# A graph attention layer: one of eight groups of x comes in turned and is normalised along the partitions

## The chip, the cores and the metric

The kernel runs on 1 core of one Trainium2 chip. The metric is the time of one execution on the device in microseconds (us); less is better.

## The reference

```python
def _layernorm(x, axis=-1, eps=1e-05):
    m = jnp.mean(x, axis=axis, keepdims=True)
    v = jnp.var(x, axis=axis, keepdims=True)
    return (x - m) / jnp.sqrt(v + eps)

h = jnp.maximum(_layernorm(x, axis=-1), 0.0)      # x: (4096, 256) f32
q = h @ Wq.T + bq
k = h @ Wk.T + bk
v = h @ Wv.T + bv
a = q @ k.T * scale + adj + adj                   # adj: (4096, 4096) f32, scale = 1/16
out = x + softmax(a, axis=-1) @ v
```

## The kernel before, in words

x has 4096 rows of 256, in 8 groups (0 to 7) of 4 tiles of 128 rows. Wq and Wk are multiplied into one matrix G, so h itself, transposed (hT, features on the partitions), takes the place of the keys. Every product is made of three f32r products of an upper and a lower part (`split_product`, 12 matmuls for 2 tiles), so h, v and q exist as "hi" and "lo".

There are 16 blocks of 256 queries and, in each, 16 units of 256 keys: 256 steps. A step makes the scores of one unit (`scores`, 12 matmuls into PSUM bank s % 2), VectorE adds adj from a ring of 23 slots (`add_adj`), and keeps a running maximum (`running_max`). Behind it come the subtraction of the maximum on GpSimd, exp and p_hi on ScalarE, p_lo on VectorE, and the product with v (`weigh_values`), 22 steps later.

The first block is woven into a prelude in which the groups of x come in, one in each turn of a loop over g. The order on each engine is written by hand. For group g it does:
- SyncE's queue (SP): `load_x(g)` into one of three buffers, and two units of adj.
- VectorE: `tile_stats` (4 bn_stats) and `part_stats` (4 bn_aggr, var + eps), three turns ahead of use; GpSimd (`make_rstd`): the power -0.5, the negated mean, their product.
- ScalarE: `normalize`, 4 activations that scale and shift the rows.
- TensorE: `transpose_h`, 8 transposes into PSUM; ScalarE `h_hi` (Relu and rounding) and VectorE `h_lo` (the rest) write hT. The part number is the group's plus 1.
- TensorE: `project_v(g, pair)`; ScalarE `v_hi` (3 instructions), GpSimd `v_lo`.
- TensorE: `scores(2g)` and `scores(2g + 1)`; before scores(s) it waits for add_adj(s - 2), whose bank it writes.

`v_hi(g, pair)` waits for `v_lo(g - 1, pair)`, since both share the buffer v_full. `project_v(g, pair)` waits for `v_hi(g - 1, pair)`. The second block's queries are projected in the turn of group 7 (`project_q(1)`, `q_hi`, `q_lo`). How many maxima each turn makes stands in a table, half of them before and half after `add_adj(2g)`:

```python
MAXES = (1, 1, 2, 4, 6, 9, 12, 2 * GROUPS - 1)
...
first, behind = MAXES[g - 1], MAXES[g]
for s in range(first, (first + behind) // 2):
    running_max(s)
...
add_adj(2 * g)
for s in range((first + behind) // 2, behind):
    running_max(s)
```

Of the kernel before, what the change touches and what calls it, by code (L numbers as in the profile page):

```python
# [5 lines left out]
def graph_attention_kernel(nc, x_groups, adj_units, w_pack, b_pack, bv, out):  # L6
# [36 lines left out]
    MAXES = (1, 1, 2, 4, 6, 9, 12, 2 * GROUPS - 1)  # L43

    term_spill = [nc.dram_tensor(f"term_spill{n}", [TILES, P], f32, kind="Internal").ap() for n in range(2)]

    ctx = ExitStack()
    with ctx:
# [5 lines left out]

        hT = sb("hT", [P, 2, DB, TILES * P], f32r)
# [22 lines left out]
        with ExitStack() as later:  # L78
            x_third = sb("x_third", [P, GT, D], f32, later)
            sb("between", [P, 3, BANK], f32, later)  # L80
            v_full = sb("v_full", [P, 2, 2, D], f32, later)
# [73 lines left out]
        s_x = [sem(f"x_rows_loaded{b}") for b in range(XB)]  # L155
        s_adj = [sem(f"adj_loaded{n}") for n in range(RING)]
# [74 lines left out]
        def _(sp):  # L231
# [53 lines left out]
            sp.wait_ge(s_ht, DB * (GROUPS - 1))  # L285
# [26 lines left out]
        def _(pool):  # L312
# [5 lines left out]
            nc.gpsimd.memset(minus_half[:, :], -0.5)  # L318
            nc.gpsimd.memset(row_terms[:, :, :], 0.0).then_inc(s_tz, 1)
# [3 lines left out]
            def make_rstd(p):  # L323
# [7 lines left out]
                if p > 1:  # L331
                    pool.wait_ge(s_off, p - 1)
                nc.gpsimd.tensor_scalar(minus_mean[:, at], mean_var[:, g % XB, at, 0], -1.0, 0.0, ALU.mult, ALU.add)\
# [4 lines left out]
                    .then_inc(s_off, 1)  # L338

# [59 lines left out]
        def _(pe):  # L399
# [190 lines left out]
        def _(act):  # L590
# [69 lines left out]
            for g in range(1, GROUPS):  # L660
                v_hi(g, 0)
                if g + 1 < GROUPS:
# [3 lines left out]
                if g + 2 < GROUPS:  # L666
                    normalize(g + 3)
                v_hi(g, 1)

# [30 lines left out]
        def _(dve):  # L700
            def tile_stats(g, j):
                if g == 0:
                    dve.wait_ge(s_x0[j], 16)
                elif j == 0:
                    dve.wait_ge(s_mv, g + 1)
                    dve.wait_ge(s_x[g % XB], 16 * (g // XB + (1 if g % XB else 0)))
                nc.vector.bn_stats(stats[:, j], rows(g)[:, j]).then_inc(s_stat, 1)

            def part_stats(p):
                g, tiles = part_of(p)  # L710
                dve.wait_ge(s_stat, GT * g + tiles[-1] + 1)
                for j in tiles:
                    last = nc.vector.bn_aggr(mean_var[:, g % XB, j], stats[:, j])
# [5 lines left out]
                nc.vector.tensor_scalar(var_eps[:, at], mean_var[:, g % XB, at, 1], EPS, 1.0, ALU.add, ALU.mult)\  # L719
                    .then_inc(s_ve, 1)  # L720

            def normalize(p):
                g, tiles = part_of(p)
                dve.wait_ge(s_rstd, p + 1)
                for j in tiles[:by_vector(p)]:
                    last = nc.vector.tensor_scalar(rows(g)[:, j], rows(g)[:, j], mean_var[:, g % XB, j, 0:1],
                                                   rstd[:, g % XB, j:j + 1], ALU.subtract, ALU.mult)
                last.then_inc(s_norm2, 1)

# [119 lines left out]
            for g in range(1, GROUPS):  # L849
# [3 lines left out]
                if g + XB < GROUPS:  # L853
# [10 lines left out]
                add_adj(2 * g)  # L864
                for s in range((first + behind) // 2, behind):
# [61 lines left out]
```

## Time and profile before

| | us |
|---|---|
| median of 3 runs | 805.5 (805.5 to 805.56) |
| profiled execution, its time | 805.57 |
| its span, first to last instruction | 803.7 |
| PE (TensorE) busy | 798.9 (99%) |
| DVE (VectorE) busy | 560.1 (70%) |
| POOL (GpSimd) busy | 412.4 (51%) |
| ACT (ScalarE) busy | 355.9 (44%) |
| granted TensorE clock | 1.00 of full speed |

The profile is one execution recorded by the hardware profiler. The span leaves out what lies ahead of the first and behind the last instruction, 1.87 us here. PEld is the load of a matmul's stationary tile, which overlaps with the matmul ahead of it. Matmuls are pipelined: an instruction starts before the shown end of the one ahead, so for a row of matmuls the distance of the starts counts. An idle time stands in brackets at the instruction that follows it, with what it waited for.

### The profile page before, as it was taken

The page shows a single profiled execution, that of the slowest core. Times are in us where ns is not written, and L with a number is a line of the kernel's source. Part 1 is how long each engine was busy: PE and PEld are TensorE (multiplying, and loading weights), DVE is VectorE, ACT ScalarE, POOL GpSimd, SP SyncE. Part 2 cuts the span into 40 slices and gives each one's busy share as a digit, 9 for nine tenths or more (in the row PEclk, how much of TensorE's full clock was granted, in tenths as well). Part 3 has the DMA queues.
Part 4 walks back from the last instruction along what each step waited for, and adds up shares of the span by engine and source line. Part 5 has one row for each costly group of instructions (what it writes and reads, how often), then busy time and mean ns, then how long its engine had stood idle before and what let it go on. Part 6 is the DMA issues. An engine that isn't in the chain of part 4 may idle for free.

```text
span 803.7 us, 16607 instructions
## 1 busy us (share of the span) xinstructions
PE 798.9 (99%) x6642; PEld 797.1 (99%) x6642; DVE 560.1 (70%) x950; ACT 355.9 (44%) x636; POOL 412.4 (51%) x369
## 2 busy tenths in 40 slices
PE   9999999999999999999999999999999999999998
PEld 8999999999999999999999999999999999999998
DVE  7869666667666766767666766767676676676664
ACT  5764444434443443434344344434444434443375
POOL 4556638091652908256190734719174380926573
PEclk9999999999999999999999999999999999999999
DMA  8522433333332434334243433323333342333300
GB/s 264 193 77 73 118 81 125 93 112 105 100 106 80 135 94 113 93 99 114 85 125 93 121 93 99 110 92 112 97 109 105 88 128 86 110 104 97 90 27 14
DMA packets 46399, 83.57 MB, mean 104 GB/s; under 512 B 5617, under 2 KB 8305, under 8 KB 46321
## 3 DMA queue, kind: packets, MB, share of 16 engines
q1 hardware_dynamic: 45744, 81.71, 34.1%
q8 instruction: 52, 0.85, 0.4%
q10 hardware_dynamic: 576, 0.79, 0.3%
q14 instruction: 27, 0.21, 0.1%
HBM read 78.25 MB, written 4.23 MB: 103 GB/s over the span
## 4 chain that ended last, share of the span: by engine, by line
PE 98%; DVE 1%; ACT 0%; issue 0%; POOL 0%; DVEq 0%; ACTq 0%; POOLq 0%
PE ps L424 51%; PE ps L535 15%; PE ps L536 15%; PE ps L537 15%; PE ps L416 1%; PE ps L402 1%; PE ps L431 0%; ACT x_pair L613 0%; DVE x_res L813 0%; DVE qhl L740 0%; DVE x_res L802 0%; ACT qhl L622 0%; POOL rstd L327 0%; DVE p_lo L793 0%; ACT G L641 0%
## 5 line engine op out<-in xcount | busy, mean ns | idle before, releaser
L424 PE MATMUL ps<-qhl,hT 128*128 128x256 f32 x3072 | 407.8, 283 | 0.6 <-DVE qhl L740 0.6
L424 PEld LDWEIGHTS ps<-qhl,hT 128*128 128x128 f32 x3072 | 383.7, 190 | 0.8 <-DVE qhl L740 0.8
L535 PE MATMUL ps<-v,p_hi 128*128 128x258 f32 x1024 | 290.6, 284 | 0.3 <-DVE p_lo L793 0.3
L536 PE MATMUL ps<-v,p_lo 128*128 128x258 f32 x1024 | 288.9, 282 | 0.0
L537 PE MATMUL ps<-v,p_hi 128*128 128x256 f32 x1024 | 288.2, 281 | 0.0
L680 ACT CAST p_hi<-ps 128x512 fp32r<-128x512 f32 x256 | 150.5, 588 | 261.5 <-PE ps L537 259.8
L392 POOL TENSOR_TENSOR ring_a<-ring_a,m_row 128x512 f32<-128x512 f32 x179 | 226.7, 1310 | 16.1 <-ACT m_row L686 15.4
L748 DVE TENSOR_TENSOR ring_a<-ps,ring_a 128x512 f32<-128x512 f32 x179 | 123.5, 691 | 117.5 <-PE ps L424 116.4
L535 PEld LDWEIGHTS ps<-v,p_hi 128*128 128x128 f32 x1024 | 194.5, 190 | 0.9 <-DVE p_lo L793 0.7
L536 PEld LDWEIGHTS ps<-v,p_lo 128*128 128x128 f32 x1024 | 194.7, 190 | 0.0
L537 PEld LDWEIGHTS ps<-v,p_hi 128*128 128x128 f32 x1024 | 193.4, 189 | 0.0
L793 DVE TENSOR_TENSOR p_lo<-ps,p_hi 128x512 fp32r<-128x512 f32 x256 | 174.4, 682 | 12.8 <-ACT p_hi L680 12.8
L674 ACT ACTIVATE ps<-ring_a 128x512 f32<-128x512 f32 x179 | 108.2, 604 | 71.3 <-DVE p_lo L793 40.8
L375 POOL PARTITION_ALL_REDUCE m_row<-max_rows x14 | 15.2, 1088 | 215.4 <-DVE max_rows L771 215.4
L392 POOL TENSOR_TENSOR ring_b<-ring_b,m_row 128x512 f32<-128x512 f32 x77 | 97.5, 1310 | 0.4
L760 DVE TENSOR_TENSOR ps<-ps,ring_a 128x512 f32<-128x512 f32 x132 | 92.2, 698 | 3.8
L748 DVE TENSOR_TENSOR ring_b<-ps,ring_b 128x512 f32<-128x512 f32 x77 | 53.2, 691 | 50.8 <-PE ps L424 50.2
L379 POOL TENSOR_TENSOR m_row<-m_row,term_row 128x256 f32<-128x256 f32 x14 | 10.2, 729 | 101.7 <-issue 101.7
L674 ACT ACTIVATE ps<-ring_b 128x512 f32<-128x512 f32 x77 | 46.5, 604 | 31.1 <-DVE p_lo L793 16.3
L760 DVE TENSOR_TENSOR ps<-ps,ring_b 128x512 f32<-128x512 f32 x63 | 44.0, 698 | 1.9
L622 ACT ACTIVATE qhl<-ps,query_bias 128x256 fp32r<-128x256 f32 x32 | 13.4, 471 | 52.3 <-PE ps L424 52.3
L343 POOL TENSOR_TENSOR v<-v_full,v 128x512 fp32r<-128x512 f32 x16 | 19.7, 1234 | 26.1 <-ACT row_terms L635 26.1
(83 smaller groups left out, 334.3 us busy)
## 6 DMA issues: line engine op xcount, KB each, us to landing
ring_a<-in_adj SPq DMA_DIRECT2D x179, 256.0 KB, 2.7
ring_b<-in_adj SPq DMA_DIRECT2D x77, 256.0 KB, 2.7
x_res<-in_x SPq DMA_DIRECT2D x16, 256.0 KB, 3.0
out<-x_res SPq DMA_DIRECT2D x15, 256.0 KB, 2.0
x_pair<-in_x SPq DMA_DIRECT2D x5, 512.0 KB, 4.2
term_row<-term_spill SPq DMA_DIRECT2D x14, 128.0 KB, 3.2
x_third<-in_x SPq DMA_DIRECT2D x2, 512.0 KB, 5.0
w_all<-in_w ACTq DMA_DIRECT2D x2, 257.0 KB, 4.0
```

Source lines behind the costliest of these rows:

```text
L343: nc.gpsimd.tensor_tensor(v[:, t:t + 2, VW:VW + D], v_full[:, pair], v[:, t:t + 2, 0:D].bitcast(f32), ALU.subtract).then_inc(s_vlo, 1)
L375: nc.gpsimd.partition_all_reduce(m_row[:, :], max_rows.ap().rearrange("p i n -> p (i n)"), P, bass.bass_isa.ReduceOp.max).then_inc(s_max, 1)
L392: nc.gpsimd.tensor_tensor(slot_tiles(w), slot_tiles(w), m, ALU.subtract).then_inc(s_sub, 1)
L424: last = nc.tensor.matmul(dst, lhs(a, ib), rhs(c, ib), start=(n == 0), stop=(n == 3 * DB - 1))
L535: nc.tensor.matmul(ps[:, at, 0:VW], hi, v[:, n, 0:VW], start=(n == 0), stop=False)
L536: nc.tensor.matmul(ps[:, at, 0:VW], lo, v[:, n, 0:VW], start=False, stop=False)
L537: last = nc.tensor.matmul(ps[:, at, 0:D], hi, v[:, n, VW:VW + D], start=False, stop=(n == TILES - 1))
L674: nc.scalar.activation(ps[:, E_BANK + w % 2, :], slot(w), ACT.Exp, scale=2.0).then_inc(s_exp, 1)
L680: nc.scalar.copy(p_hi[:, w % PB], bank_tiles(E_BANK + w % 2)).then_inc(s_phi, 1)
L748: nc.vector.tensor_tensor(slot(s), ps[:, S_BANK + s % 2, :], slot(s), ALU.add).then_inc(s_add, 1)
L760: last = nc.vector.tensor_tensor(to, first, slot(s), ALU.max)
L793: nc.vector.tensor_tensor(p_lo[:, w % PB], bank_tiles(E_BANK + w % 2), p_hi[:, w % PB].bitcast(f32), ALU.subtract).then_inc(s_plo, 1)
```

## The change

Group 7 alone (LATE = 7) is no longer transposed on TensorE. The host hands over a second, transposed copy of its x (`in_xt`). Its plain rows are loaded into the place of hT's upper part for that group, and serve for the statistics; the turned rows are loaded into the place of the lower part. GpSimd puts 1/sqrt(var + eps) and the mean of the 512 rows side by side (`gather_moments`), VectorE turns them in blocks of 32x32, SP writes them to DRAM in four pieces (`spill_moments`) and reads each of the two rows of 512 values back to all 128 partitions (`load_key_row`, 256 KB each). GpSimd subtracts the means (`centre`), VectorE takes the maximum with 0 and multiplies (`scale_late`), ScalarE rounds to hi, VectorE writes lo (`late_lo`). In MAXES one maximum of the turn g = 3 moves to g = 4. In the code `make_rstd`, `normalize`, `transpose_h` and the PSUM forms of `h_hi` and `h_lo` are no longer called for group 7.

```diff
-def graph_attention_kernel(nc, x_groups, adj_units, w_pack, b_pack, bv, out):
+def graph_attention_kernel(nc, x_groups, x_turned, adj_units, w_pack, b_pack, bv, out):
...
-    MAXES = (1, 1, 2, 4, 6, 9, 12, 2 * GROUPS - 1)
-
+    LATE = GROUPS - x_turned.shape[0]
+    ROWS = 3
+    MAXES = (1, 1, 2, 3, 6, 9, 12, 2 * GROUPS - 1)
+
+    row_spill = [nc.dram_tensor(f"row_spill{n}", [2 * GT, P], f32, kind="Internal").ap() for n in range(GROUPS - LATE)]
...
+            h_plain = sb("h_plain", [P, 2, DB, TILES * P], f32, unsplit)
...
-            sb("between", [P, 3, BANK], f32, later)
+            key_rows = sb("key_rows", [P, ROWS, GT * P], f32, later)
...
+        def key_row(g, a):
+            n = 2 * (g - LATE) + a
+            return key_rows[:, n % ROWS, :].rearrange("p (one n) -> p one n", one=1).broadcast_to([P, DB, GT * P])
+
+        def rows_loaded(g, a):
+            n = 2 * (g - LATE) + a
+            return s_row[n % ROWS], 16 * (n // ROWS + 1)
+
+        def x_tile(g, j):
+            if g < LATE:
+                return rows(g)[:, j]
+            return h_plain[:, 0, j // 2, (g * GT + j % 2 * 2) * P:(g * GT + j % 2 * 2 + 2) * P]
...
+            def load_late(g):
+                sp.dma_start(plain_keys(0, g), x_groups[g].rearrange("p (b t) d -> p b (t d)", b=DB))\
+                    .then_inc(s_xn[g - LATE], 16)
+
+            def load_turned(g):
+                sp.dma_start(plain_keys(1, g), x_turned[g - LATE]).then_inc(s_xt[g - LATE], 16)
+
+            def spill_moments(g):
+                n = g - LATE
+                sp.wait_ge(s_mturn, n + 1)
+                for c in range(P // 32):
+                    sp.dma_start(row_spill[n][:, 32 * c:32 * c + 32], moments_turned[32 * c:32 * c + 2 * GT, n])\
+                        .then_inc(s_rsp[n], 16)
+
+            def load_key_row(g, a):
+                n = 2 * (g - LATE) + a
+                sp.wait_ge(s_rsp[g - LATE], 16 * (P // 32))
+                if n >= ROWS:
+                    sp.wait_ge((s_cen, s_hf)[(n - ROWS) % 2], (n - ROWS) // 2 + 1)
+                sp.dma_start(key_rows[:, n % ROWS, :], bass.AP(row_spill[g - LATE].tensor, a * GT * P, [[0, P], [1, GT * P]]))\
+                    .then_inc(s_row[n % ROWS], 16)
...
-            for g in range(2, GROUPS):
+            for g in range(2, LATE):
                 load_x(g)
                 load_adj(2 * g - 2)
                 load_adj(2 * g - 1)
+                if LATE <= g + 2 < GROUPS:
+                    load_late(g + 2)
+            for g in range(LATE, GROUPS):
+                load_turned(g)
+                load_adj(2 * g - 2)
+                spill_moments(g)
+                load_adj(2 * g - 1)
+                for a in range(2):
+                    load_key_row(g, a)
             for s in range(2 * GROUPS - 2, FIRST):
                 load_adj(s)
 
             sp.wait_ge(s_glo, 1)
             sp.wait_ge(s_bmm, 1)
-            sp.wait_ge(s_ht, DB * (GROUPS - 1))
+            sp.wait_ge(s_hf, GROUPS - LATE)
+            sp.wait_ge(s_ht, DB * (LATE + 1))
...
+            def gather_moments(p):
+                g = part_of(p)[0]
+                n = g - LATE
+                pool.wait_ge(s_ve, p + 1)
+                pool.wait_ge(s_mz, 1)
+                nc.gpsimd.tensor_tensor(moments[:, n, GT:2 * GT], var_eps[:, :], minus_half[:, :], ALU.pow).then_inc(s_rstd, 1)
+                nc.gpsimd.tensor_scalar(moments[:, n, 0:GT], moments_of(g)[:, :, 0], 1.0, 0.0, ALU.mult, ALU.add)\
+                    .then_inc(s_mean, 1)
+
+            def centre(g):
+                pool.wait_ge(s_xt[g - LATE], 16)
+                pool.wait_ge(*rows_loaded(g, 0))
+                x_turned_here = plain_keys(1, g)
+                nc.gpsimd.tensor_tensor(x_turned_here, x_turned_here, key_row(g, 0), ALU.subtract).then_inc(s_cen, 1)
...
+                if g + XB == LATE - 1:
+                    make_rstd(g + XB + 1)
+                    gather_moments(g + XB + 2)
+                if g + XB == LATE:
+                    centre(LATE)
                 v_lo(g, 1)
-                if g + XB < GROUPS:
+                if g + XB < LATE - 1:
...
                 project_v(g, 0)
-                if g + 1 < GROUPS:
+                if g + 1 < LATE:
...
+                if g >= LATE:
+                    act.wait_ge(s_hf, g - LATE + 1)
+                    nc.scalar.copy(keys_of(0, g), plain_keys(1, g)).then_inc(s_hhi, 1)
+                    return
...
                 v_hi(g, 0)
-                if g + 1 < GROUPS:
+                if g + 1 < LATE:
                     h_hi(g + 2)
                 if g == Q1_GROUP:
                     q_hi(1)
-                if g + 2 < GROUPS:
+                if g + 2 < LATE:
                     normalize(g + 3)
                 v_hi(g, 1)
+                if g == LATE - 2:
+                    h_hi(LATE + 1)
...
+            def turn_moments(g):
+                n = g - LATE
+                dve.wait_ge(s_rstd, g + 2)
+                dve.wait_ge(s_mean, n + 1)
+                nc.vector.transpose(moments_turned[:, n], moments[:, n]).then_inc(s_mturn, 1)
+
+            def scale_late(g):
+                dve.wait_ge(s_cen, g - LATE + 1)
+                dve.wait_ge(*rows_loaded(g, 1))
+                x_turned_here = plain_keys(1, g)
+                nc.vector.scalar_tensor_tensor(x_turned_here, x_turned_here, 0.0, key_row(g, 1), ALU.max, ALU.mult)\
+                    .then_inc(s_hf, 1)
+
+            def late_lo(g):
+                dve.wait_ge(s_hhi, g + 2)
+                nc.vector.tensor_tensor(keys_of(1, g), plain_keys(1, g), keys_of(0, g).bitcast(f32),
+                                        ALU.subtract).then_inc(s_hlo, 1)
...
+                early = g + XB if g + XB < LATE else g + XB + 1
+                if early < GROUPS:
                     for j in range(GT):
-                        tile_stats(g + XB, j)
-                    part_stats(g + XB + 1)
-                if 1 < g < GROUPS - 1:
+                        tile_stats(early, j)
+                    part_stats(early + 1)
+                if LATE <= early - 1 < GROUPS:
+                    turn_moments(early - 1)
+                if 1 < g < LATE - 1:
                     h_lo(g + 2)
+                if g == LATE - 2:
+                    scale_late(LATE)
+                elif g == LATE - 1:
+                    late_lo(LATE)
                 first, behind = MAXES[g - 1], MAXES[g]
                 for s in range(first, (first + behind) // 2):
                     running_max(s)
                 if g == Q1_GROUP:
                     q_lo(1)
                 add_adj(2 * g)
+                if g + XB + 1 == LATE:
+                    for j in range(GT):
+                        tile_stats(LATE, j)
+                    part_stats(LATE + 1)
...
+        "in_xt": np.ascontiguousarray(x.reshape(-1, GT * P, d // P, P).transpose(0, 3, 2, 1)[LATE:]),
```

VectorE, from the end of the turn g = 3 of the loop to the middle of g = 4 (`stats` to `var_eps` is tile_stats and part_stats; L866 is add_adj, L878 running_max, L852 h_lo). Before:

```order
L748 TENSOR_TENSOR ring_a<-ps,ring_a 128x512 [waits adj_loaded5,scores_done]
...
L734 SCALAR_TENSOR_TENSOR hT<-ps,hT 128x2x512 [waits h_hi_written]
L760 TENSOR_TENSOR acc<-acc,ring_a 128x512 [waits first_block_max_kept,logits_written]
L748 TENSOR_TENSOR ring_a<-ps,ring_a 128x512 [waits adj_loaded6,scores_done]
L760 TENSOR_TENSOR acc<-acc,ring_a 128x512 [waits first_block_max_kept,logits_written]
L748 TENSOR_TENSOR ring_a<-ps,ring_a 128x512 [waits adj_loaded7,scores_done]
```

and now:

```order
L866 TENSOR_TENSOR ring_a<-ps,ring_a 128x512 [waits adj_loaded5,scores_done]
...
L852 SCALAR_TENSOR_TENSOR hT<-ps,hT 128x2x512 [waits h_hi_written]
L866 TENSOR_TENSOR ring_a<-ps,ring_a 128x512 [waits adj_loaded6,scores_done]
L807 BN_STATS stats<-h_plain 128x6 [waits late_x_rows_loaded0,mean_var_ready]
...
L819 TENSOR_SCALAR var_eps<-mean_var 128x4 [waits rstd_ready,mean_var_ready]
L878 TENSOR_TENSOR acc<-acc,ring_a 128x512 [waits first_block_max_kept,logits_written]
L866 TENSOR_TENSOR ring_a<-ps,ring_a 128x512 [waits adj_loaded7,scores_done]
L834 STREAM_TRANSPOSE moments_turned<-moments 128x32 [waits means_gathered,rstd_ready]
```

The statistics of group 7 stand behind add_adj(6), where before they stood behind add_adj(7), and the transpose of the moments follows add_adj(7).

VectorE, turns g = 5 and g = 6, now:

```order
L866 TENSOR_TENSOR ring_a<-ps,ring_a 128x512 [waits adj_loaded9,scores_done]
L852 SCALAR_TENSOR_TENSOR hT<-ps,hT 128x2x512 [waits h_hi_written]
L840 SCALAR_TENSOR_TENSOR h_plain<-h_plain,key_rows 128x2x512 [waits key_row_loaded1,late_x_centred]
L878 TENSOR_TENSOR acc<-acc,ring_a 128x512 [waits first_block_max_kept,logits_written]
L866 TENSOR_TENSOR ring_a<-ps,ring_a 128x512 [waits adj_loaded10,scores_done]
...
L866 TENSOR_TENSOR ring_a<-ps,ring_a 128x512 [waits adj_loaded11,scores_done]
L845 TENSOR_TENSOR hT<-h_plain,hT 128x2x512 [waits h_hi_written]
```

scale_late (L840) is new, with its wait, ahead of running_max(6) and add_adj(10); late_lo (L845) stands where h_lo of group 7 stood, behind add_adj(11).

GpSimd, turns g = 3 to g = 5, now (L398 to L408 is make_rstd, L429 v_lo):

```order
L429 TENSOR_TENSOR v<-v_full,v 128x2x256 [waits v_hi_written]
L398 TENSOR_TENSOR rstd<-var_eps,minus_half 128x4 [waits var_eps_ready]
L404 TENSOR_SCALAR minus_mean<-mean_var 128x4 [waits offset_ready]
L408 TENSOR_TENSOR offset<-minus_mean,rstd 128x4 [waits rstd_ready,minus_mean_ready]
L416 TENSOR_TENSOR moments<-var_eps,minus_half 128x4 [waits moments_zeroed,var_eps_ready]
L417 TENSOR_SCALAR moments<-mean_var 128x4
L429 TENSOR_TENSOR v<-v_full,v 128x2x256 [waits v_hi_written] x2
L424 TENSOR_TENSOR h_plain<-h_plain,key_rows 128x2x512 [waits key_row_loaded0,late_x_turned_loaded0]
L429 TENSOR_TENSOR v<-v_full,v 128x2x256 [waits v_hi_written] x7
```

make_rstd of group 6 and the moments of group 7 stand ahead of v_lo(3,1), before they stood behind it and behind v_lo(4,1). centre (L424) and its wait are new between v_lo(4,0) and v_lo(4,1).

## Rows read from the trace of the kernel before

**Rows 1.** The page: engines' busy time, and the chain that ended last

```profile
PE 798.9 (99%) x6642; PEld 797.1 (99%) x6642; DVE 560.1 (70%) x950; ACT 355.9 (44%) x636; POOL 412.4 (51%) x369
...
PE 98%; DVE 1%; ACT 0%; issue 0%; POOL 0%; DVEq 0%; ACTq 0%; POOLq 0%
```

**Rows 2.** PE in order of time: start, us, engine, line, operation, count

```profile
53.80 1.03 PE L416 MATMUL ps<-ident,x_pair 128*128 128x128 f32 x8
54.60 1.68 PE L424 MATMUL ps<-qhl,hT 128*128 128x256 f32 x12
...
57.55 1.60 PE L424 MATMUL ps<-qhl,hT 128*128 128x256 f32 x12
58.99 1.60 PE L424 MATMUL ps<-wv_T,hT 128*128 128x258 f32 x12
...
61.86 4.48 PE L424 MATMUL ps<-qhl,hT 128*128 128x256 f32 x36
```

**Rows 3.** DVE in order of time, the prelude from 38 us on

```profile
38.06 0.68 DVE L748 TENSOR_TENSOR ring_a<-ps,ring_a 128x512 f32<-128x512 f32 x1
...
39.92 1.40 DVE L707 BATCH_NORM_STATS2 stats<-x_pair 128x6 f32<-128x256 f32 x4
...
41.77 0.17 DVE L719 TENSOR_SCALAR var_eps<-mean_var 128x4 f32<-128x4 f32 x1
42.94 1.22 DVE L734 SCALAR_TENSOR_TENSOR hT<-ps,hT 128x1024 fp32r<-128x1024 f32 x1 [1.00 <-ACT hT L603]
...
51.30 0.68 DVE L748 TENSOR_TENSOR ring_a<-ps,ring_a 128x512 f32<-128x512 f32 x1
...
53.30 0.20 DVE L789 STREAM_TRANSPOSE terms_turned<-row_terms 128x32 f32<-128x32 f32 x1
...
62.93 0.88 DVE L740 SCALAR_TENSOR_TENSOR qhl<-ps,query_bias,qhl 128x256 fp32r<-128x256 f32 x2 [0.91 <-ACT qhl L622]
63.73 0.68 DVE L748 TENSOR_TENSOR ring_a<-ps,ring_a 128x512 f32<-128x512 f32 x1
```

**Rows 4.** POOL in order of time, the same stretch

```profile
40.60 1.00 POOL L327 TENSOR_TENSOR rstd<-var_eps,minus_half 128x4 f32<-128x4 f32 x1
41.59 0.19 POOL L333 TENSOR_SCALAR minus_mean<-mean_var 128x4 f32<-128x4 f32 x1
...
46.06 1.20 POOL L343 TENSOR_TENSOR v<-v_full,v 128x512 fp32r<-128x512 f32 x1 [2.79 <-ACT row_terms L635]
```

**Rows 5.** Narrow windows: DVE and POOL instructions that meet in SBUF

```profile
52.69 1.75 POOL L343 TENSOR_TENSOR v<-v_full,v 128x512 fp32r<-128x512 f32 x1 [2.80 <-ACT row_terms L635]
52.69 0.69 DVE L760 TENSOR_TENSOR acc<-acc,ring_a 128x512 f32<-128x512 f32 x1
...
59.06 1.21 POOL L343 TENSOR_TENSOR v<-v_full,v 128x512 fp32r<-128x512 f32 x1 [2.55 <-ACT row_terms L635]
59.32 1.50 DVE L760 TENSOR_TENSOR acc<-acc,ring_a 128x512 f32<-128x512 f32 x1
```

**Rows 6.** SP; landings of L256, L248, L235; POOL lines (ns, min/median/max)

```profile
53.53 1.74 SPq L248 DMA_DIRECT2D term_spill<-terms_turned  x4
...
DMA to landing us min/median/max: 3.0/3.2/4.0
...
DMA to landing us min/median/max: 1.3/1.4/3.2
...
DMA to landing us min/median/max: 2.4/2.7/6.7
...
L379 POOL TENSOR_TENSOR m_row<-m_row,term_row x14: 725/729/736, 114.7 to 730.6; 128x256 f32<-128x256 f32 x14
...
L392 POOL TENSOR_TENSOR ring_a<-ring_a,m_row x179: 1282/1306/1840, 70.3 to 789.0; 128x512 f32<-128x512 f32 x179
```

**Rows 7.** POOL's start; a window: us, busy by engine, PEclk, DMA share, GB/s

```profile
6.14 1.04 POOL L327 TENSOR_TENSOR rstd<-var_eps,minus_half 128x2 f32<-128x2 f32 x1 [4.04 <-DVE var_eps L719]
...
12.00:14.00 2.00, 1.40 (x12) 1.16 (x11) 1.38 (x7) 1.62 (x6) 1.39 (x3) 1.00 0.91 361
```

More of the change, by code:

```diff
@@ L53, in sem @@
             return ctx.enter_context(nc.semaphore(name))
+        with ExitStack() as unsplit:
+            h_plain = sb("h_plain", [P, 2, DB, TILES * P], f32, unsplit)
         hT = sb("hT", [P, 2, DB, TILES * P], f32r)
@@ L88, in graph_attention_kernel @@
             stats = sb("stats", [P, GT, 6], f32, prelude)
-            mean_var = sb("mean_var", [P, XB, GT, 2], f32, prelude)
+            mean_var = sb("mean_var", [P, XB + 2, GT, 2], f32, prelude)
+            moments = sb("moments", [P, 2, 32], f32, prelude)
+            moments_turned = sb("moments_turned", [P, 2, 32], f32, prelude)
             var_eps = sb("var_eps", [P, GT], f32, prelude)
@@ L119, in rows, with moments_of, keys_of, plain_keys @@
             return x_third[:, :, :] if g % XB == 2 else x_pair[:, g % XB]
+        def moments_of(g):
+            return mean_var[:, g % XB if g < LATE else XB + g - LATE]
+        def keys_of(a, g):
+            return hT[:, a, :, g * GT * P:(g + 1) * GT * P]
+        def plain_keys(a, g):
+            return h_plain[:, a, :, g * GT * P:(g + 1) * GT * P]
+        def key_row(g, a):
[8 more added lines that the diff above has]
+            return h_plain[:, 0, j // 2, (g * GT + j % 2 * 2) * P:(g * GT + j % 2 * 2 + 2) * P]
         def part_of(p):
@@ L155, in graph_attention_kernel @@
         s_x = [sem(f"x_rows_loaded{b}") for b in range(XB)]
+        s_xn = [sem(f"late_x_rows_loaded{n}") for n in range(GROUPS - LATE)]
+        s_xt = [sem(f"late_x_turned_loaded{n}") for n in range(GROUPS - LATE)]
+        s_row = [sem(f"key_row_loaded{n}") for n in range(ROWS)]
+        s_rsp = [sem(f"moments_spilled{n}") for n in range(GROUPS - LATE)]
+        s_mz = sem("moments_zeroed")
+        s_mean = sem("means_gathered")
+        s_mturn = sem("moments_turned_around")
+        s_cen = sem("late_x_centred")
+        s_hf = sem("late_h_written")
         s_adj = [sem(f"adj_loaded{n}") for n in range(RING)]
@@ L318, in _ @@
             nc.gpsimd.memset(minus_half[:, :], -0.5)
+            nc.gpsimd.memset(moments[:, :, :], 0.0).then_inc(s_mz, 1)
             nc.gpsimd.memset(row_terms[:, :, :], 0.0).then_inc(s_tz, 1)
@@ L332, in make_rstd @@
                     pool.wait_ge(s_off, p - 1)
-                nc.gpsimd.tensor_scalar(minus_mean[:, at], mean_var[:, g % XB, at, 0], -1.0, 0.0, ALU.mult, ALU.add)\
+                nc.gpsimd.tensor_scalar(minus_mean[:, at], moments_of(g)[:, at, 0], -1.0, 0.0, ALU.mult, ALU.add)\
                     .then_inc(s_mm, 1)
@@ L703, in tile_stats @@
                     dve.wait_ge(s_x0[j], 16)
+                elif j == 0 and g >= LATE:
+                    dve.wait_ge(s_mv, g + 1)
+                    dve.wait_ge(s_xn[g - LATE], 16)
                 elif j == 0:
@@ L706, in tile_stats @@
                     dve.wait_ge(s_x[g % XB], 16 * (g // XB + (1 if g % XB else 0)))
-                nc.vector.bn_stats(stats[:, j], rows(g)[:, j]).then_inc(s_stat, 1)
+                nc.vector.bn_stats(stats[:, j], x_tile(g, j)).then_inc(s_stat, 1)
             def part_stats(p):
@@ L712, in part_stats @@
                 for j in tiles:
-                    last = nc.vector.bn_aggr(mean_var[:, g % XB, j], stats[:, j])
+                    last = nc.vector.bn_aggr(moments_of(g)[:, j], stats[:, j])
                 last.then_inc(s_mv, 1)
@@ L718, in part_stats @@
                 at = slice(tiles[0], tiles[-1] + 1)
-                nc.vector.tensor_scalar(var_eps[:, at], mean_var[:, g % XB, at, 1], EPS, 1.0, ALU.add, ALU.mult)\
+                nc.vector.tensor_scalar(var_eps[:, at], moments_of(g)[:, at, 1], EPS, 1.0, ALU.add, ALU.mult)\
                     .then_inc(s_ve, 1)
@@ L725, in normalize @@
                 for j in tiles[:by_vector(p)]:
-                    last = nc.vector.tensor_scalar(rows(g)[:, j], rows(g)[:, j], mean_var[:, g % XB, j, 0:1],
+                    last = nc.vector.tensor_scalar(rows(g)[:, j], rows(g)[:, j], moments_of(g)[:, j, 0:1],
                                                    rstd[:, g % XB, j:j + 1], ALU.subtract, ALU.mult)
                 last.then_inc(s_norm2, 1)
+            def turn_moments(g):
[13 more added lines that the diff above has]
+                                        ALU.subtract).then_inc(s_hlo, 1)
             def h_lo(p):
@@ L893 @@
     from concourse.bass_utils import run_bass_kernel_spmd
-    P, QB, KT, GT = 128, 256, 2, 4
+    P, QB, KT, GT, LATE = 128, 256, 2, 4, 7
     x = np.asarray(inputs["x"])
```

1 line of the change is left out of this document (removed).

## The prediction

> **What bounds the kernel now.** I read the page first. TensorE (PE) is busy for 798.9 of 803.7 us, and 98% of the chain that ended last is PE [rows 1]. So only two things can move the time: fewer or shorter PE instructions, or PE waiting where it does not wait now. The profiled execution took 805.57 us, 1.87 more than its span, and the median of the runs is 805.5; I add changes to 805.57 and take 0.07 off at the end.
>
> Then PE's instructions in order of time, over the loop in which the x groups come in [rows 2]. No idle time stands in a bracket there. The work of group 7 is the 8 transposes at 53.80; scores(12) follow at 54.60, scores(13) at 57.55, project_v(7,0) at 58.99, and three pairs of score products, scores(14) to scores(16), from 61.86 on. PE is the clock for all others: what these steps need must be there when their turn comes. scores(12) needs add_adj(10) (a PSUM bank is reused every second step), scores(13) needs add_adj(11), project_v(7,0) needs the lower half of h of group 7, scores(16) needs add_adj(14), which stands behind q_lo(1) on VectorE (DVE).
>
> **What is taken off PE.** The 8 transposes show 1.03 us, but matmuls overlap; by starts they take 54.60 - 53.80 = 0.80 us [rows 2]. That is the whole direct gain, 0.1%, and since PE is the bound it counts in full. Every later need of PE comes 0.80 us earlier: scores(12) at 53.80, scores(13) at 56.75, project_v(7,0) at 58.19.
>
> **What is taken off elsewhere** is worth nothing by itself: normalize(8), h_hi(8) and h_lo(8) of group 7 are work beside PE, and the new h_hi and late_lo, with as many elements, take their place (h_lo 1.22 us, [rows 3]). The added memset stands at POOL's start, where it idles for 4.04 us before its first power [rows 7]; without that cover it would cost its own length, which is that of the memset of row_terms beside it, of the same shape.
>
> **The new chain, step by step.**
> 1. add_adj(6) moves ahead of running_max(2), which takes 0.60 by the starts, so it begins at 37.46, not 38.06. The statistics of group 7 follow at 38.06 and take 2.02 (from 39.92 to 41.77 + 0.17): done at 40.08 [rows 3]. Its x was requested behind x of group 5, two turns of 6.6 us earlier, so it is there. add_adj(7) comes 1.3 later, and scores(9), which need it, are two products behind scores(8): hidden.
> 2. POOL: power 1.00 and the means 0.19 [rows 4], starting 0.08 later: done at 41.34. v_lo(3,1), which stood right ahead of the power at 40.60, now waits behind, some 2 us. v_hi(4,1), a turn later on ScalarE, waits for it: hidden.
> 3. The transpose on DVE takes 0.20 [rows 3]: done at 41.6.
> 4. SP issues four spills, 1.74 us in all, the last some 1.3 after the first, and each lands 1.3 to 3.2 (median 1.4) later [rows 6]: 44.35. Behind them on SP stand adj 13 to 15, which DVE wants only after scores(13) at 57.55, and the ring loads of slots 16 to 20, which now wait for scale_late, until some 53 us. The first of those is wanted after scores(16), over 12 us later, and 6.7 is the longest landing of such a load [rows 6]: hidden.
> 5. The key row of the means, a broadcast of 2 KB to 128 partitions. No row has it. Nearest is term_row, the same kind at half the size: 3.0 to 4.0, median 3.2; a plain load of 256 KB has 2.7 [rows 6]. Bounds: 3.0 below (a larger transfer is not faster), 4.4 above (4.0 and 0.4 for the bytes). I take 3.4, near the median: it lands at 47.8.
> 6. centre on POOL, 128x1024. POOL took 729 ns for 256 elements and 1306 for 512 with a spread operand [rows 6], 2.25 ns for one more, so 2.46 us (v_lo's 1.20 doubled gives 2.4, 1306 doubled 2.6). It ends at 50.25. All this time v_lo(4,1), which ran at 46.06 [rows 4], stands behind it, and v_lo(5,0) behind that, ready too.
> 7. Now both queues want SBUF at once. When a DVE instruction with two operands in SBUF meets a POOL one, one waits for the other's end: running_max took 1.50 instead of 0.69 us beside v_lo, and v_lo 1.75 instead of 1.20 beside running_max [rows 4, 5]. A DVE instruction that reads PSUM does not suffer: h_lo at 42.94 kept its 1.22 beside a v_lo. And the one that waits gets its turn between two of the other's: v_lo at 59.06, in its own 1.21, went in between two maxima [rows 3, 5]. scale_late and late_lo have both inputs in SBUF, and scale_late waits for centre. POOL starts its own next instruction just before the shown end of the last (41.59, behind 40.60 + 1.00, [rows 4]), while DVE must first see the semaphore, so v_lo(4,1) goes first: to 51.45. Then scale_late (about 1.15, as h_lo of the same size) to 52.6, then v_lo(5,0), which has waited, to 53.8, then running_max(6) to 54.4, then add_adj(10) to 55.1. In the kernel before it was over at 51.98 [rows 3]. PE wants it at 53.80: **a wait of 1.3 us**.
> 8. v_lo(5,1) to 55.6, running_max(7) to 56.2, v_lo(6,0) to 57.4, running_max(8) to 58.0, the small transpose, add_adj(11) to 58.8. PE wants it at 56.75 + 1.3 = 58.05: **0.75 more**. late_lo is done at 59.95, wanted at 60.2: met, by little.
> 9. q_lo(1) had 0.91 us of idle DVE before it, and add_adj(14) behind it was over at 64.41, 0.33 before scores(16) at 61.86 + 2 x 1.44 = 64.74 [rows 2, 3]. Counting on, two more maxima each wait for a v_lo, and DVE comes about 1.2 late to q_lo(1). So the wait lies between 0 and 0.9. I take the middle, **0.45**.
>
> Sum: 1.3 + 0.75 + 0.45 - 0.80 = +1.7. The main loop (DVE busy 70%, POOL 51%, [rows 1]) is as before and gives nothing back, since PE has no slack to recover in. 805.57 + 1.7 - 0.07 = 807.2.
>
> The Trainium skill ("SBUF — State Buffer", section "SBUF: two separate sides") calls this port pair an exclusive lock that is held for a whole instruction, and counts every DVE operation with two SBUF inputs; rows 5 agree, and that scalar_tensor_tensor falls under it stands only there. Were it exempt, scale_late would end at 51.45 and the sum would be near that of the second rival.
>
> The Trainium skill ("DMA: Bandwidth & Descriptors", section "Anatomy of one DMA") gives a fixed part of about 2.0 us and bytes over 436 GB/s. By that the spill would take 2.0 and a key row 2.6, together 0.2 less than my 1.4 + 3.4, and the estimate would be 807.0; the spill's 1.4 in the trace speaks against it.
>
> **The rivals.**
> - *The rows land later still.* With 4.0 to 4.4 for the key row, or a spill nearer its 3.2, centre ends 0.6 to 1.2 later, and so does each step behind it: 807.8 to 808.4. For it: the broadcast is 256 KB and term_row reached 4.0. Against: little else moves then, as the ring loads now wait for scale_late.
> - *DVE gets the port first.* Then scale_late ends at 51.4, v_lo(4,1) at 52.6, running_max(6) at 53.2, add_adj(10) at 53.9: a wait of 0.1. add_adj(11) ends at 57.6 against 56.85: 0.75. With 0.2 for the third place the sum is +0.25: 805.8. For it: at 52.69 both began together and DVE won [rows 5].
> - *Hidden, the other side.* If add_adj(10) and (11) are over in time, only the 0.80 is left: 804.7. The point from which it decides: centre must be over by 49.0, 1.25 earlier than by my sum, with two v_lo ahead of add_adj(10), and by 50.2 with one. For it: the queue is empty at 42 us, and two landings of 4.8 us together are my largest term. Against: the shortest of the rows, 1.3 and 3.0, save only 0.5.
> - *PE's clock falls* in its new pauses. The granted clock stayed 1.00 through the 0.60 us of idle time in the stretch from 12 to 14 us (PE busy 1.40 of 2.00, [rows 7]), and the pauses here are of that order. If it fell, over 808.6.
>
> **How the numbers follow.** Forecast 0.40, late rows 0.25, DVE first 0.20, hidden 0.12, clock 0.03. About 0.2% (1.6 us) is what a measurement can tell from no change. The forecast's 807.2 lies at this bound (807.1), so half of it, 0.20, counts as slower, with late rows 0.25 and clock 0.03: 0.48. Same: 0.20, DVE first 0.20 and 0.10 of hidden: 0.50. Faster: 0.02, where something more than the 0.80 were gained. The range from 804.7 to 808.3 takes in all but the clock and the top of the late rows. The forecast's own range is 806.3 to 807.9 (landings 3.0 to 4.0, third wait 0 to 0.9).
>
> **What would show it.** PE with 56 transposes instead of 64. Idle time on PE before scores(12) of 1 to 2 us, released by DVE's add_adj(10), and again before scores(13). scale_late or a running_max with a duration of 1.2 us above its own. centre at 47 to 49 us. Wrong: PE without any wait between 50 and 66 us (hidden), or the wait being released by ScalarE (v_hi(5,1) late behind v_lo(4,1)) or by late_lo.

## The result and the profile after

The changed kernel takes 807.73 us (median of 14 runs) against 805.53 for the kernel before in the same comparison: ratio 1.003, 95% interval 1.0023 to 1.0037. It is 2.2 us slower, where 1.7 were predicted (807.2), inside the range. Thirteen of the 14 runs lie between 807.12 and 808.42; the last took 811.59 at a mean granted clock of 0.994, and no trace of it was kept.

The page of the changed kernel: engines, then the chain.

```profile
PE 798.2 (99%) x6634; PEld 795.4 (99%) x6634; DVE 564.9 (70%) x952; ACT 353.9 (44%) x632; POOL 416.1 (52%) x370
...
PE 94%; DVE 2%; issue 1%; DMA 1%; ACT 1%; POOL 1%; SPq 0%; ACTq 0%; DVEq 0%; POOLq 0%
```

PE has 8 matmuls fewer and its busy time fell by 0.7 us, yet the span grew by 2.0 (803.7 to 805.7). The chain was PE for 98% [rows 1]; now it passes through VectorE, DMA and GpSimd. Where, PE in order of time shows (start, us, operation; in brackets the idle time ahead):

```profile
52.55 1.60 PE L515 MATMUL ps<-wv_T,hT 128*128 128x258 f32 x12
55.49 1.70 PE L515 MATMUL ps<-qhl,hT 128*128 128x256 f32 x12 [1.34 <-DVE ring_a L866]
...
58.77 1.69 PE L515 MATMUL ps<-qhl,hT 128*128 128x256 f32 x12
...
63.17 3.04 PE L515 MATMUL ps<-qhl,hT 128*128 128x256 f32 x24
66.52 1.66 PE L515 MATMUL ps<-qhl,hT 128*128 128x256 f32 x12 [0.31 <-DVE ring_a L866]
```

These stand for the rows of PE in [rows 2]. The transposes at 53.80 are gone. scores(12) starts at 55.49, where 52.55 + 1.44 = 53.99 was possible: 1.50 us of waiting by the starts (the bracket counts from the modelled end, so it is smaller). From scores(12) to scores(13) it is 3.28 where it was 2.95: 0.33 more. scores(16) could start at 63.17 + 2.88 = 66.05: 0.47. The balance: -0.80 + 1.50 + 0.33 + 0.47 is 1.5; 0.19 more is there from the start on (the first load of weights landed that much later in this execution, and everything is shifted by it), and the rest, 0.26, is 0.08 behind scores(13), 0.05 behind scores(16) and 0.13 at turn_max(0), whose max_rows is late. Together they are the 2.0 of the span.

Why VectorE is late, from GpSimd and VectorE in order of time:

```profile
40.33 1.39 POOL L416 TENSOR_TENSOR moments<-var_eps,minus_half 128x4 f32<-128x4 f32 x1 [2.08 <-DVE var_eps L819]
...
48.59 2.40 POOL L424 TENSOR_TENSOR h_plain<-h_plain,key_rows 128x1024 f32<-128x1024 f32 x1 [4.39 <-DMA key_rows<-row_spill]
50.95 6.52 POOL L429 TENSOR_TENSOR v<-v_full,v 128x512 fp32r<-128x512 f32 x4
```

```profile
51.03 2.20 DVE L840 SCALAR_TENSOR_TENSOR h_plain<-h_plain,key_rows 128x1024 f32<-128x1024 f32 x1
53.16 1.68 DVE L878 TENSOR_TENSOR acc<-acc,ring_a 128x512 f32<-128x512 f32 x1
54.76 0.68 DVE L866 TENSOR_TENSOR ring_a<-ps,ring_a 128x512 f32<-128x512 f32 x1
55.36 2.66 DVE L878 TENSOR_TENSOR acc<-acc,ring_a 128x512 f32<-128x512 f32 x2
```

GpSimd waits 4.39 us for the key row of the means, while v_lo(4,1) (which ran at 46.06 before, [rows 4]) stands behind the waiting centre. Then it has four v_lo to do at once: 6.52 us for 4 x 1.20 of work. VectorE's scale_late starts 0.08 after the first of them and takes 2.20, running_max(6) 1.68, running_max(7) and (8) 2.66. The durations fit two queues that take turns, each v_lo pushing one instruction of VectorE back (the rows merge the four v_lo, so the moments of the handovers are worked out, not seen). add_adj(10) (54.76) is itself not slowed; it stands behind.

The round trip over DRAM, from the chain of work in order of time (the four pieces are written, then the row of the means is read back):

```profile
43.29 1.16 DMA row_spill<-moments_turned
...
44.46 4.00 DMA key_rows<-row_spill
```

### The profile page after: what moved, and what is told of

Same layout as the page of the kernel before. It is cut to its first block, busy times and chain, and to the rows that moved or that the text cites. A ratio compares the mean times of both kernels' runs of the same rounds, so it can differ in the third digit from the quotient of the medians.

```text
span 805.7 us, 16600 instructions
## 1 busy us (share of the span) xinstructions
PE 798.2 (99%) x6634; PEld 795.4 (99%) x6634; DVE 564.9 (70%) x952; ACT 353.9 (44%) x632; POOL 416.1 (52%) x370
## 4 chain that ended last, share of the span: by engine, by line
PE 94%; DVE 2%; issue 1%; DMA 1%; ACT 1%; POOL 1%; SPq 0%; ACTq 0%; DVEq 0%; POOLq 0%
PE ps L515 48%; PE ps L626 15%; PE ps L627 15%; PE ps L628 15%; DVE acc L878 1%; DMA w_all<-in_w 1%; DMA key_rows<-row_spill 0%; PE ps L507 0%; POOL h_plain L424 0%; PE ps L522 0%; DVE ring_a L866 0%; DVE qhl L858 0%; POOL moments L416 0%; DVE stats L807 0%; DVE hT L845 0%
## 5 line engine op out<-in xcount | busy, mean ns | idle before, releaser
L866 DVE TENSOR_TENSOR ring_a<-ps,ring_a 128x512 f32<-128x512 f32 x179 | 123.4, 690 | 117.6 <-PE ps L515 116.5
L878 DVE TENSOR_TENSOR ps<-ps,ring_a 128x512 f32<-128x512 f32 x132 | 92.1, 698 | 3.8
L866 DVE TENSOR_TENSOR ring_b<-ps,ring_b 128x512 f32<-128x512 f32 x77 | 53.2, 690 | 50.8 <-PE ps L515 50.2
L878 DVE TENSOR_TENSOR ps<-ps,ring_b 128x512 f32<-128x512 f32 x63 | 44.0, 698 | 1.9
L858 DVE SCALAR_TENSOR_TENSOR qhl<-ps,query_bias,qhl 128x256 fp32r<-128x256 f32 x32 | 14.0, 480 | 23.3 <-ACT qhl L717 23.3
```

The source lines that it names most:

```text
L858: last = nc.vector.scalar_tensor_tensor(qhl[:, b % 2, 1, ob, :], q_at(b, ob), query_bias[:, ob:ob + 1], qhl[:, b % 2, 0, ob, :].bitcast(f3 ...
L866: nc.vector.tensor_tensor(slot(s), ps[:, S_BANK + s % 2, :], slot(s), ALU.add).then_inc(s_add, 1)
L878: last = nc.vector.tensor_tensor(to, first, slot(s), ALU.max)
```

## The experiments

The rival theories: (a) the round trip over DRAM makes the chain late; (b) meetings of VectorE and GpSimd in SBUF hold VectorE up; (c) VectorE simply has too much to do there; (d) it is only the order of the instructions. Each kernel ran 11 times, in between runs of the kernel before (805.29, 805.4 and 805.5 in the three comparisons: e1 to e4, e5 to e7, e8 to e10), so I compare with the one of the same comparison. The 95% intervals of the ratios are some 0.7 us wide on either side, about as much as the 8 transposes are worth; for differences of that size the rows of the trace are the better evidence.

**e1, the key rows early.** Group 7's values are wrong here: the rows come from x.

```diff
             for g in range(LATE, GROUPS):
                 load_turned(g)
+                for a in range(2):
+                    load_key_row(g, a)
...
-                sp.wait_ge(s_rsp[g - LATE], 16 * (P // 32))
-                sp.dma_start(key_rows[:, n % ROWS, :], bass.AP(row_spill[g - LATE].tensor, a * GT * P, [[0, P], [1, GT * P]]))\
+                sp.dma_start(key_rows[:, n % ROWS, :], bass.AP(x_groups.tensor, a * GT * P, [[0, P], [1, GT * P]]))\
...
```

> The two key rows are loaded from x itself right behind the turned rows, ahead of the spills, so that centre waits for no round trip; every instruction of the changed kernel is still there. It leaves out the mean and the scale of group 7 (the rows hold other values). If the round trip over DRAM (4 us of waiting on GpSimd) is what makes scale_late late, PE waits neither before scores(12) nor before scores(13), about 1.7 of the lost time comes back and only what VectorE is late at scores(16) may remain: 804.9 to 805.4. If the added work and the meetings in SBUF cost the time whatever the rows do, the wait before scores(12) stays at 1 us or more and the time at 807 or more.

Measured: 805.07 against 805.29 (ratio 0.9996, 0.9987 to 1.0005). All work and all traffic are there, and the waits at scores(12) and scores(13) are gone. VectorE and PE:

```profile
50.76 1.22 DVE L840 SCALAR_TENSOR_TENSOR h_plain<-h_plain,key_rows 128x1024 f32<-128x1024 f32 x1
...
61.00 1.56 DVE L878 TENSOR_TENSOR acc<-acc,ring_a 128x512 f32<-128x512 f32 x1
```

```profile
64.09 1.66 PE L515 MATMUL ps<-qhl,hT 128*128 128x256 f32 x12 [0.31 <-DVE ring_a L866]
```

scale_late takes 1.22, alone. So (c) falls, and (a) carries the first two waits. Only 0.2 of the 0.8 is won, though: running_max(12) meets v_lo(7,0), takes 1.56, and PE waits at scores(16).

**e2, centre behind v_lo(4,1)** on GpSimd.

```diff
-                if g + XB == LATE:
-                    centre(LATE)
                 v_lo(g, 1)
+                if g + XB == LATE:
+                    centre(LATE)
```

> centre stands behind v_lo(4,1) instead of ahead of it, so this v_lo runs in the time in which GpSimd waits for the rows. If the queue of v_lo behind centre is the point (GpSimd always has another v_lo ready when scale_late and running_max(6) want SBUF), the wait before scores(12) hardly changes (1.3 to 1.5 us), since v_lo(5,0) and v_lo(5,1) take the same places, and the gain comes only later, one v_lo less before scores(13) and scores(16): 0.5 to 0.8 us in all, 807.0 to 807.2. If it were that single v_lo which holds scale_late up, the wait before scores(12) falls by 1.1 and the time is about 806.5 or less. If neither matters, 807.7.

Measured: 807.19 against 805.29 (1.0023, 1.0014 to 1.0032), the time that the first theory had. The wait at scores(12) did not fall; by the starts it is 1.84, above the 1.3 to 1.5 expected, because the first key row landed after 4.36 instead of 4.00 in this execution:

```profile
55.63 1.70 PE L515 MATMUL ps<-qhl,hT 128*128 128x256 f32 x12 [1.69 <-DVE ring_a L866]
```

v_lo(5,0) takes the place of the v_lo that moved, and scale_late is 2.20 again. The shorter queue pays only later: from scores(12) to scores(13) it is 2.98, nearly the 2.95 of before again.

**e3, scale_late with one input in PSUM.** It leaves out the values of group 7.

```diff
-                nc.vector.scalar_tensor_tensor(x_turned_here, x_turned_here, 0.0, key_row(g, 1), ALU.max, ALU.mult)\
+                stale = ps[:, HT_BANK:HT_BANK + DB, 0:GT * P]
+                nc.vector.scalar_tensor_tensor(x_turned_here, stale, 0.0, key_row(g, 1), ALU.max, ALU.mult)\
```

> scale_late reads its first input from PSUM (what is left there of group 6) instead of the centred rows in SBUF; waits, place and size are the same. It leaves out the values of group 7. If two inputs in SBUF are what makes it wait for GpSimd, its duration falls from 2.20 to about 1.2 us, it ends about 1 us earlier, running_max(6) then has the wait (for v_lo(4,1) instead of v_lo(5,0)) and the wait before scores(12) falls to 0.2 to 0.5 us: 806.2 to 806.9. If its 2.20 us are its own (a slow form on rows spread over two halves), nothing changes: 807.7.

Measured: 806.01 against 805.29 (1.0008, 0.9999 to 1.0016).

```profile
51.06 1.23 DVE L841 SCALAR_TENSOR_TENSOR h_plain<-ps,key_rows 128x1024 f32<-128x1024 f32 x1 [0.54 <-POOL h_plain L424]
52.20 1.69 DVE L879 TENSOR_TENSOR acc<-acc,ring_a 128x512 f32<-128x512 f32 x1
```

At the same place and size, with v_lo beside it, scale_late takes 1.23 instead of 2.20: its second microsecond was the wait for GpSimd. running_max(6), with both inputs in SBUF, still has its own (1.69). scores(12) then waits 1.01 by the starts, more than the 0.2 to 0.5 expected: the 1.50 did lose the microsecond of scale_late, but the first key row landed after 4.50 in this execution instead of 4.00, which gives half of it back. scores(13) no longer waits, so the total came out a little better than expected.

**e4, the first block's maximum in PSUM** from unit 6 on.

```diff
-                kept = acc[:, :] if b == 0 else ps[:, A_BANK, :]
-                first = slot(s - 1) if u == 1 else kept
-                to = acc[:, :] if u == UNITS - 1 else kept
+                def kept_at(n):
+                    if b == 0:
+                        return acc[:, :] if n < TO_PSUM else ps[:, HT_BANK, :]
+                    return ps[:, A_BANK, :]
+
+                if s == TO_PSUM:
+                    dve.wait_ge(s_hlo, LATE + 1)
+                first = slot(s - 1) if u == 1 else kept_at(u - 1)
+                to = acc[:, :] if u == UNITS - 1 else kept_at(u)
```

HT_BANK is one of the banks into which the transposes wrote; it is free by then.

> From running_max(6) on, the first block's running maximum is kept in PSUM bank 2, free by then, so running_max(7) to (15) have one input in SBUF and one in PSUM; running_max(6) still has two in SBUF. If the meetings in SBUF make the later waits, the wait before scores(12) stays (1.3 to 1.5 us), those before scores(13) and scores(16) vanish (1.0 to 1.3 us in all): 806.4 to 806.8. If VectorE is simply too full there, nothing is won, or a little is lost to the slower PSUM operand: 807.7 to 808.

Measured: 806.32 against 805.29 (1.0012, 1.0003 to 1.0021). PE and VectorE:

```profile
55.85 1.69 PE L516 MATMUL ps<-qhl,hT 128*128 128x256 f32 x12 [1.60 <-DVE ring_a L867]
...
63.12 4.48 PE L516 MATMUL ps<-qhl,hT 128*128 128x256 f32 x36
```

```profile
55.72 1.49 DVE L885 TENSOR_TENSOR ps<-ps,ring_a 128x512 f32<-128x512 f32 x2
```

running_max(7) and (8) take 1.49 for both instead of 2.66, beside the same v_lo. Every wait behind scores(12) is gone, scores(14) to (16) are one piece of 4.48 as in [rows 2], and the wait at scores(12) stays (1.76 by the starts; the key row landed after 4.26).

**e5, the additions first.**

```diff
+                if g != LATE - 1:
+                    add_adj(2 * g - 1)
...
                 if g == LATE - 2:
+                    add_adj(2 * g)
                     scale_late(LATE)
-                elif g == LATE - 1:
-                    late_lo(LATE)
+                    add_adj(2 * g + 1)
...
```

In the lines left out, late_lo is put behind running_max(6), and the add_adj(10) of the old place is dropped.

> On VectorE add_adj(10) moves ahead of scale_late and add_adj(11) right behind it, and one maximum ahead of late_lo; nothing is added or taken away. If PE's waits before scores(12) and scores(13) are only the place of the two additions behind blocked instructions, both vanish. But the maxima that meet GpSimd stay and are late: VectorE comes late to add_adj(12), (13) or (14), so waits before scores(14) to scores(16) take their place, 2 to 2.8 us in all, and the time stays within 0.8 us of the changed kernel (807.0 to 807.8). If the order is all there is to it, 804.8 to 805.2.

Measured: 807.16 against 805.4 (1.0022, 1.0013 to 1.0031). The waits moved instead of going away:

```profile
61.59 1.70 PE L515 MATMUL ps<-qhl,hT 128*128 128x256 f32 x12 [0.59 <-DVE ring_a L866]
64.10 1.69 PE L515 MATMUL ps<-qhl,hT 128*128 128x256 f32 x12 [0.80 <-DVE ring_a L866]
66.17 1.67 PE L515 MATMUL ps<-qhl,hT 128*128 128x256 f32 x12 [0.39 <-DVE ring_a L866]
```

By the starts 0.75, 1.07 and 0.63, at scores(14), (15) and (16). Order alone (d) is not it: the time for which VectorE is held up has to be paid somewhere, by whichever addition stands behind it.

**e6, all three** (e2, e4 and e5 together; it computes the full reference).

> The three rearrangements together: centre behind v_lo(4,1), add_adj(10) and (11) early, the running maximum in PSUM from unit 6 on. Every theory of the meetings in SBUF says that PE then waits nowhere between 50 and 68 us and only the saving of the 8 transposes is left: 0.80 less than before, 804.7 to 804.9. If a wait for late_lo or for v_hi takes their place, 805.2 to 806.5.

Measured: 804.63 against 805.4 (0.999, 0.9981 to 0.9999). It is 0.8 us below the kernel before, about what the 8 transposes take on PE, though the interval only just leaves 1 out. VectorE and PE:

```profile
51.44 1.81 DVE L841 SCALAR_TENSOR_TENSOR h_plain<-h_plain,key_rows 128x1024 f32<-128x1024 f32 x1
```

```profile
53.93 1.60 PE L516 MATMUL ps<-qhl,hT 128*128 128x256 f32 x12
55.37 1.60 PE L516 MATMUL ps<-wv_T,hT 128*128 128x258 f32 x12
56.80 1.60 PE L516 MATMUL ps<-qhl,hT 128*128 128x256 f32 x12
...
61.12 4.48 PE L516 MATMUL ps<-qhl,hT 128*128 128x256 f32 x36
```

The key rows come as late as in the changed kernel and scale_late is still held up (1.81), but add_adj(10) now stands ahead of it, and what stands behind it (add_adj(11), late_lo) is in time for PE.

**e7, the transposes of group 7 left out of the kernel before**, with no chain in their place. Its h of group 7 is that of group 6.

```diff
+                if p == GROUPS:
+                    return
                 for ib in range(DB):
                     for j in tiles:
...
```

In the lines left out, `h_hi` of group 7 no longer waits for the transposes, but for project_v(6,0) and h_lo of group 6; it starts where it did before (55.26, with this execution's shift of 0.15; 55.12).

> The kernel before with the 8 transposes of group 7 simply left out (h of group 7 is then that of group 6), with no new chain. It measures what the transposes are worth on PE by themselves: 0.80 us by the starts, so 804.7. If they were partly hidden (another engine sets the pace behind them), 805.0 to 805.5; if the load of the identity and the switch cost more than the starts show, 804.4.

Measured: 805.37 against 805.4 (0.9998, 0.9989 to 1.0007). This is the surprise: by the medians the saving alone is worth nothing. PE here, and its product behind scores(12) in the kernel before:

```profile
53.95 1.60 PE L426 MATMUL ps<-qhl,hT 128*128 128x256 f32 x12
55.39 1.60 PE L426 MATMUL ps<-wv_T,hT 128*128 128x258 f32 x12
...
61.13 3.04 PE L426 MATMUL ps<-qhl,hT 128*128 128x256 f32 x24
64.48 1.67 PE L426 MATMUL ps<-qhl,hT 128*128 128x256 f32 x12 [0.31 <-DVE ring_a L753]
```

```profile
56.12 1.60 PE L424 MATMUL ps<-wv_T,hT 128*128 128x258 f32 x12
```

From scores(12) to that product it is 1.44 here and 1.52 in the kernel before (54.60, [rows 2]), so the transposes are worth 0.88 and not 0.80. But scores(16) starts 0.47 later than it could (61.13 + 2.88 = 64.01), and 0.18 more go behind it, up to turn_max(0): 0.65 of the 0.88 are given back. This execution also began 0.15 later, as the first load of weights landed later; the 0.1 to 0.2 us that are left are too little for the medians to show.

VectorE and then GpSimd here:

```profile
61.40 1.55 DVE L765 TENSOR_TENSOR acc<-acc,ring_a 128x512 f32<-128x512 f32 x1
```

```profile
61.21 1.19 POOL L343 TENSOR_TENSOR v<-v_full,v 128x512 fp32r<-128x512 f32 x1 [1.67 <-ACT row_terms L640]
```

And in the kernel before:

```profile
61.34 0.68 DVE L760 TENSOR_TENSOR acc<-acc,ring_a 128x512 f32<-128x512 f32 x1
```

```profile
61.94 1.20 POOL L343 TENSOR_TENSOR v<-v_full,v 128x512 fp32r<-128x512 f32 x1 [1.67 <-ACT row_terms L635]
```

GpSimd's v_lo(7,0) follows PE's products behind the transposes and so comes 0.73 us earlier. VectorE does not: from h_lo of group 7 on, which hangs on work ahead of the transposes, it is busy without a break. In the kernel before, v_lo(7,0) began when running_max(12) was all but done, and ran in the gap ahead of q_lo(1) (the 0.91 in [rows 3]). Now it begins ahead of running_max(12), and that waits for it.

**e8, the kernel before with the maximum in PSUM** from unit 9 on (the diff of e4, with TO_PSUM = 9 and a wait for h_lo of group 7, which frees the bank), and **e9, the same in e7**.

> The kernel before, with the first block's running maximum kept in PSUM from unit 9 on (bank 2 is free there only behind h_lo of group 7). PE waits for nothing in the kernel before, so a VectorE that is less held up changes nothing: 805.3 to 805.5, equal to before. If the PSUM form were faster in some way of its own, or if VectorE cost the kernel before something unseen, 804.5 to 805.1.

> The same in the kernel without the 8 transposes of group 7 (its h is that of group 6). Leaving them out alone won nothing (805.37 against 805.4): in its profile running_max(12) is held up by v_lo(7,0), 1.55 us, and PE waits at scores(16) and before turn_max. If that meeting eats the saving, it is gone here and the 0.80 us show in full: 804.5 to 804.8. If the transposes are worth nothing on PE, 805.3.

Measured: e8 805.6, e9 804.6, against 805.5 (ratios 1.0001, 0.9992 to 1.001, and 0.9989, 0.998 to 0.9998). By the medians, relief for VectorE is worth nothing alone, the transposes are worth nothing alone, and together they are worth 0.9. The wait at scores(16) is gone in e9:

```profile
60.96 4.48 PE L427 MATMUL ps<-qhl,hT 128*128 128x256 f32 x36
```

e9 has no transposes and no new chain either (group 7 keeps its old statistics, normalize, h_hi and h_lo), and is hardly faster than e6, which has the chain: 0.9 below its kernel before against 0.8. In the traces turn_max(0) stands at 66.90 in e6 and 66.74 in e9, and e6 began its products 0.15 later from the start on. So in e6 the new chain is hidden.

**e10, e6 with centre left ahead of v_lo(4,1).**

> The early additions and the maximum in PSUM, with centre left ahead of v_lo(4,1) as in the changed kernel. If the position of centre is only a refinement, GpSimd being late by one v_lo holds up late_lo and running_max(6) a little: a wait of 0 to 0.5 us at scores(16), 804.7 to 805.2. If the v_lo chain of GpSimd is the next bound once VectorE is free (v_hi(5,1) waits for v_lo(4,1), project_v(6,1) for v_hi(5,1)), 805.5 or more.

Measured: 804.98 against 805.5 (0.9994, 0.9985 to 1.0003). PE's three score products from 60.79 on take 4.74 instead of 4.48, and late_lo is held up to 2.21:

```profile
60.79 4.74 PE L516 MATMUL ps<-qhl,hT 128*128 128x256 f32 x36
```

On VectorE:

```profile
54.71 2.21 DVE L846 TENSOR_TENSOR hT<-h_plain,hT 128x1024 fp32r<-128x1024 f32 x1
```

So the place of centre is worth some 0.2 to 0.3 once the rest is right (the intervals of e6 and e10 overlap, so the size is not settled; the row shows the wait). Other places for v_lo, or a faster way for the rows than over DRAM, were not tried.

## Why the prediction was right, and where not

The mechanism came true: a late centre, scale_late and the maxima held up by v_lo, PE waiting for the additions behind them. Of the four terms of the sum, the first two waits were right for the reason given; the saving and the third wait were not.

*The saving* (0.80, "counts in full"). Its size on PE was nearly right (0.88, e7), that it counts in full was wrong. e7 shows that the kernel before gives most of it back, 0.65, 0.47 of it at scores(16), through a meeting of running_max(12) and v_lo(7,0) that did not exist before. The step "PE is the bound, so it counts in full" overlooks that the queues that follow PE are shifted against each other. The sum did not suffer, because a third wait (0.45) was counted, but it was put down to the new chain. The wait at scores(16) is the same 0.47 without the chain (e7) and with the chain in time (e1), so that the two numbers met was luck.

*Steps 1 to 3.* The statistics were done at 40.25, predicted 40.08; the difference is the shift of 0.19. The power took 1.39 instead of 1.00 beside running_max(2), which I had not seen coming; the moments were turned at 42.2 instead of 41.6.

*Steps 4 and 5.* The spills went out in 1.35 instead of 1.74 and landed after 1.16, below the shortest of [rows 6] (1.3); that took back the 0.4 that the power had lost. The key rows landed after 4.0 and 4.9, where 3.4 was taken: the term that was mis-sized, at the edge of what term_row had shown [rows 6]. It is the rival of the late rows, half way, and with it centre ended at 50.99 instead of 50.25 (0.19 of it the shift). It also explains most of what is missing between the profiled execution (1.8 without its shift) and the median (2.2), as far as single executions can tell: the first row landed after 4.36, 4.50 and 4.26 in those of e2, e3 and e4, whose way up to there is that of the changed kernel but for one v_lo in e2. The Trainium skill ("DMA: Bandwidth & Descriptors", section "Anatomy of one DMA") states its fixed 2.0 us for DMAs that GpSimd issues, while these are issued on SyncE's queue. With the bytes it would have given, as an estimate, about 2.6 for the row and 2.0 for the spill; the trace has 4.0 and 1.16, so both are off, in opposite directions.

*Step 6.* centre took 2.40, predicted 2.46.

*Step 7.* v_lo(4,1) first, scale_late held up, then v_lo(5,0), running_max(6), add_adj(10): the order was as predicted, and the wait 1.50 instead of 1.3. e3 and e4 show the mechanism one instruction at a time. The Trainium skill ("SBUF — State Buffer", section "SBUF: two separate sides") counts every VectorE operation with two SBUF inputs, and so scalar_tensor_tensor; e3 agrees, with 2.20 against 1.23. centre ended 0.55 later than predicted (without the shift), but from there to the end of add_adj(10) it took 4.45 instead of 4.85, since each instruction starts a little before the shown end of the one ahead; two errors partly cancelled, and 1.3 came out nearer than its terms were. The rival in which VectorE is served first did not happen in any of the profiles.

*Step 8.* 0.33 instead of 0.75. The two waits together are 1.83, predicted 2.05: running_max(7) and (8) took 2.66, where I had counted 2.9 (55.1 to 58.0). *Step 9.* 0.47, predicted 0.45, for another reason, as said. The granted clock stayed at 1.00 in the profiled execution, also from 54 to 56 us, where PE was busy for only 0.66 us.

*The range.* "Landings 3.0 to 4.0, third wait 0 to 0.9" gives 806.3 to 808.25 by the prediction's own terms, not 807.9. The 807.73 lies inside either.

## What to carry to other kernels

A chain may be late without harm if nothing that the bound engine needs stands behind it in any queue: order by need first, then ask what the held-up instructions do to the ones behind. Before something is taken off the bound engine, look at the engines that follow it: a saving shifts them against each other, and here a new meeting ate 0.65 of 0.88 us until one operand was moved to PSUM. Two kinds of relief that each show nothing can be worth their full sum together (e7, e8 and e9), so test them together before either is dropped.

## What the runs showed of the hardware

- VectorE instructions with both inputs in SBUF and the GpSimd instructions of this kernel hold each other up: 2.20, 1.68 and 2.66 (for two) of VectorE beside v_lo, and with both queues full the durations fit a strict alternation, one instruction each. With one input in PSUM VectorE is not held up: 1.23 (e3) and 1.49 for two (e4).
- Even a GpSimd power over 128x4 elements pays for it: 1.39 beside running_max(2), instead of 1.00 us.
- A broadcast of 2 KB from DRAM to 128 partitions landed 4.0 and 4.9 us after its issue in this kernel, where a plain load of 256 KB had a median of 2.7. That the broadcast is the cause is not shown: the plain loads of 256 KB issued just behind it landed after 5.1 and 5.3 us, so the traffic of that moment may be it.
